# Transposes of the softmax tiles held back by two row tiles instead of one, with a third probability buffer and one bank wait per row tile, in an 8-core attention and FFN layer

## What is computed

```python
xn = layernorm(x)
q_a = rmsnorm(xn @ w_q_a);  q = (q_a @ w_q_b).reshape(s, 16, 128 + 64)
ckv_kpe = xn @ w_kv_a                      # 512 latent + 64 rope
ckv = rmsnorm(ckv_kpe[..., :512]);  k_pe = rope(ckv_kpe[..., 512:])
q_abs = einsum('shd,rhd->shr', q_nope, w_uk)          # 16 heads, 512 wide
scores = (concat(q_abs, rope(q_pe)) @ concat(ckv, k_pe).T) * 192**-0.5
attn = softmax(where(causal, scores, min))
o_ckv = einsum('hqk,kr->qhr', attn, ckv)
y = einsum('qhr,hre->qe', o_ckv, w_uv @ w_o)
out = x + y + (silu(xn @ w_gate.T) * (xn @ w_up.T)) @ w_down.T
```

## Time and profile before

| | us |
|---|---|
| Median of the runs | 7982.84 |
| Lowest and highest of the 2 runs | 7969.11, 7996.58 |
| Profiled execution, its time | 7445.65 |
| Profiled execution, span of the slowest core | 7443.9 |
| Spans of all cores in it | 7394.0 to 7443.9 |
| TensorE matmul, busy in the span | 5451.9 (73%) |
| VectorE, busy | 1725.5 (23%) |
| ScalarE, busy | 1211.8 (16%) |

### The profile page before, as it was taken

One profiled execution on the slowest core, in us unless ns is written; L12 is line 12 of the kernel. 1 busy time (PEld: TensorE's weight loads), 2 busy tenths in 40 slices (PEclk: granted clock), 3 DMA queues, 4 the chain that ended last, 5 costly groups with the idle time before them and its releaser, 6 DMA issues. The chain is left out here.

```text
span 7443.9 us, 70098 instructions; the slowest of 8 cores (7394.0 to 7443.9 us)
## 1 busy us (share of the span) xinstructions
PE 5451.9 (73%) x24376; PEld 2381.6 (32%) x24856; DVE 1725.5 (23%) x4676; ACT 1211.8 (16%) x2788; POOL 366.0 (5%) x408
## 2 busy tenths in 40 slices
PE   3345546666666766667777779976998699869987
PEld 1222222222222222223333334432443244324433
DVE  3323334414332333223333300000000000000000
ACT  0000102213322333223333200000000000000000
POOL 0000002211111010000000000000000000000000
PEclk7666767778888888888888889998999899989999
DMA  3331139998758553453333176645664566446643
GB/s 90 79 62 23 24 57 161 150 134 104 101 80 126 78 80 66 74 103 62 61 61 62 35 178 153 150 127 170 153 153 125 168 153 152 129 158 158 152 130 122
DMA packets 2101325, 819.71 MB, mean 110 GB/s; under 512 B 1819763, under 2 KB 2073844, under 8 KB 2094838
## 3 DMA queue, kind: packets, MB, share of 16 engines
q1 hardware_dynamic: 1621814, 627.20, 33.3%
q0 software_dynamic: 479168, 188.02, 22.3%
HBM read 854.20 MB, written 148.90 MB: 135 GB/s over the span
## 5 line engine op out<-in xcount | busy, mean ns | idle before, releaser
L1040 PE MATMUL ps<-wd,h_sb 128*128 128x512 bf16 x4014 | 930.7, 386 | 236.0 <-DMA wd<-wdown_bf 197.0
L988 PE MATMUL ps<-fx,wg 128*128 128x512 bf16 x4015 | 934.9, 383 | 152.4 <-DMA wg<-wgup_bf 85.1
L764 PE MATMUL ps<-kT,qf 128*128 128x512 bf16 (+3 forms) x2473 | 711.1, 419 | 295.7 <-DVE qf L691 183.1
L996 PE MATMUL ps<-fx,wg 128*128 128x512 bf16 x4013 | 919.7, 379 | 4.4
L1040 PEld LDWEIGHTS ps<-wd,h_sb 128*128 128x128 bf16 x4096 | 394.6, 99 | 772.2 <-issue 348.1
L834 PE MATMUL ps<-ptasm,ckv_nat 128*128 128x512 bf16 (+3 forms) x2502 | 563.2, 389 | 74.8 <-DVE ptasm L725 72.5
L988 PEld LDWEIGHTS ps<-fx,wg 128*128 128x128 bf16 x4096 | 404.1, 99 | 644.0 <-issue 171.2
L1011 DVE TENSOR_TENSOR h_sb<-sil,ps 128x512 bf16<-128x512 f32 x256 | 176.1, 688 | 1801.7 <-PE ps L996 1801.7
L996 PEld LDWEIGHTS ps<-fx,wg 128*128 128x128 bf16 x4096 | 400.8, 98 | 483.3
L800 ACT ACTIVATE p_nat<-s_stage,e_bias 128x512 bf16<-128x512 f32 (+3 forms) x640 | 414.2, 648 | 618.0 <-DVE e_bias L795 618.0
L714 PE MATMUL pt<-ident_sb,p_nat 128*128 128x128 bf16 x2176 | 208.3, 254 | 395.4 <-DVE ptasm L725 298.0
(11 more groups left out here) (102 smaller groups left out, 3082.5 us busy)
## 6 DMA issues: line engine op xcount, KB each, us to landing
wg<-wgup_bf SPq DMA_DIRECT2D x512, 512.0 KB, 4.1
wd<-wdown_bf SPq DMA_DIRECT2D x256, 512.0 KB, 3.9
conv<-wgup POOLq DMA_DIRECT2D x128, 512.0 KB, 10.8
wgup_bf<-conv SPq DMA_DIRECT2D x128, 512.0 KB, 8.2
wo<-wo POOLq DMA_DIRECT2D x16, 2048.0 KB, 23.4
conv<-wdown POOLq DMA_DIRECT2D x64, 512.0 KB, 9.9
wdown_bf<-conv SPq DMA_DIRECT2D x64, 512.0 KB, 6.1
wnope<-wqbnope POOLq DMA_DIRECT2D x64, 384.0 KB, 5.6
```

What stands on the lines that cost most here:

```text
L764: lhs=lhs, rhs=rhs: e.matmul(bank[:, 0:w], lhs(e), rhs(e), start=(cc == 0), stop=(cc == 4)),
L988: b.op("tensor", lambda e, gs=gs, ec=ec, s_g=s_g, pg=pg: e.matmul(pg[:, :], wg_sb[s_g][:, ec * 128:(ec + 1) * 128], xnt_g[gs][:, ec * 512: ...
L996: b.op("tensor", lambda e, gs=gs, ec=ec, s_u=s_u, pu=pu: e.matmul(pu[:, :], wg_sb[s_u][:, ec * 128:(ec + 1) * 128], xnt_g[gs][:, ec * 512: ...
L1040: banks=banks: e.matmul(banks[tt4][:, :], h_sb[:, ic * 512 + tt4 * 128:ic * 512 + (tt4 + 1) * 128], wd_sb[isl][:, (ic % 4) * 512:(ic % 4 + ...
```

## The change

Transposes are now held in a list and emitted when more than two are pending, so those of row tile i-2 stand behind the scores and the scaling of row tile i, and two of them are left for the end of the head. `p_nat` gets a third buffer for that. The three bank waits of a row tile's first three score groups are put together into one, ahead of its first matmul; the fourth group of block 3 keeps its own.

```diff
-            p_nat = [psb(f"p_nat{i}", [128, S], BF16) for i in range(2)]
+            p_nat = [psb(f"p_nat{i}", [128, S], BF16) for i in range(3)]
...
-                    pend_tr = None
+                    pend_tr = []
...
+                        b.waits("tensor", [(V, v_qf), (V, qpeT_ready), (V, kT_ready)]
+                                + [ps_free[1 + (sbank + gg) % 3]
+                                   for gg in range(min(G, 3))])
                         for g in range(G):
                             w = (min(4 * g + 4, n_k) - 4 * g) * 128
                             pk = 1 + (sbank % 3)
                             sbank += 1
                             bank = PS[pk]
-                            b.waits("tensor", [(V, v_qf), ps_free[pk],
-                                               (V, qpeT_ready), (V, kT_ready)])
+                            if g >= 3:
+                                b.waits("tensor", [ps_free[pk]])
...
-                        if pend_tr is not None:
-                            emit_transposes(*pend_tr)
-                        pend_tr = (i, n_k, v_pn)
+                        pend_tr.append((i, n_k, v_pn))
+                        if len(pend_tr) > 2:
+                            emit_transposes(*pend_tr.pop(0))
                     if h < 15:
                         s_qn_tok[1 - hs] = emit_qnope(h + 1)
-                    emit_transposes(*pend_tr)
+                    while pend_tr:
+                        emit_transposes(*pend_tr.pop(0))
```

More of the change, by code:

```diff
@@ L600, in build_nc @@
             ptasm_free = None
-            p_nat_free = [None, None]
+            p_nat_free = [None, None, None]
             qf_free = [None, None]
@@ L715, in emit_transposes @@
                                 PT[pb][:, slot * 128:(slot + 1) * 128],
-                                p_nat[i % 2][:, kc * 128:(kc + 1) * 128], ident[:, :],
+                                p_nat[i % 3][:, kc * 128:(kc + 1) * 128], ident[:, :],
                                 is_transpose=True, start=(slot == 0), stop=last),
@@ L732, in emit_transposes @@
                                 pt_free[pb] = (V, b.cnt[V])
-                        p_nat_free[i % 2] = (T, t_tr_done)
+                        p_nat_free[i % 3] = (T, t_tr_done)
                         pt_evac_v = b.cnt[V]
@@ L796, in build_nc @@
                             e_bias[:, :], mx_row[:, :], -SM, None, ALU.mult), V)
-                        b.waits("scalar", [(V, v_bias), p_nat_free[i % 2]])
+                        b.waits("scalar", [(V, v_bias), p_nat_free[i % 3]])
                         for g in range(G):
@@ L800, in build_nc @@
                             b.op("scalar", lambda e, g=g, w=w, i=i: e.activation(
-                                p_nat[i % 2][:, 4 * g * 128:4 * g * 128 + w],
+                                p_nat[i % 3][:, 4 * g * 128:4 * g * 128 + w],
                                 s_stage[:, 4 * g * 128:4 * g * 128 + w],
@@ L815, in build_nc @@
                         v_pn = b.op("vector", lambda e, n_k=n_k, i=i: e.tensor_scalar(
-                            p_nat[i % 2][:, 0:n_k * 128], p_nat[i % 2][:, 0:n_k * 128],
+                            p_nat[i % 3][:, 0:n_k * 128], p_nat[i % 3][:, 0:n_k * 128],
                             sm_inv[:, :], None, ALU.mult), V)
-                        if pend_tr is not None:
-                            emit_transposes(*pend_tr)
-                        pend_tr = (i, n_k, v_pn)
+                        pend_tr.append((i, n_k, v_pn))
+                        if len(pend_tr) > 2:
+                            emit_transposes(*pend_tr.pop(0))
                     if h < 15:
                         s_qn_tok[1 - hs] = emit_qnope(h + 1)
-                    emit_transposes(*pend_tr)
+                    while pend_tr:
+                        emit_transposes(*pend_tr.pop(0))
                     qf_free[hs] = (T, last_S_T)
```

## The result

| | before | changed |
|---|---|---|
| median of all runs, us | 7690.72 (29 runs) | 7619.57 (30 runs) |
| lowest and highest | 7428.65, 8043.56 | 7487.85, 8131.95 |
| profiled execution, us | 7445.65 | 7496.27 |

The changed kernel takes 1.0083 times as long, 95% interval 1.0071 to 1.0095: slower, by 0.8%, although its median in the table is the lower one. In many executions of either kernel, both runs of before in the table ahead of the prediction among them, the cores of one die or both had a lower clock and took up to 9% longer, so the medians hold a mixture of both kinds, and the ratio leaves such executions out. The predicted ratio, 8059 / 7983 = 1.0095, lies at the upper end of the interval. The predicted time, 8059, was not met: 7619.57 lies outside 7965 to 8165.

A forecast was written before the change was run, and what follows sets the result against it. It took the ScalarE-VectorE ring through s_stage and the copies behind the last scaling to bound attention. Block terms of 10.4 + 12.8 + 28.8 + 24.0 made +76 us, added to 7982.84 for 8059; range 7965 to 8165.

The forecast's parts named there:

- the carry to the median: Whole kernel: the +76 us added unscaled to the timed median 7982.84, giving 8059, though the profiled execution was 7445.65.
- The sum: Attention, 16 heads a block: +0.65, +0.8, +1.8 and +1.5 us a head in blocks 0 to 3, together +76 us.
- Part 1: Scores of row tiles 2 and 3 come earlier: gain of 0.45 us a head in block 0, 0.8 in block 1.
- Part 2: Behind the last scaling, one more transpose-and-copy step: loss of 1.1, 1.6, 1.8, 1.5 us a head in blocks 0 to 3.
- Part 3: Joined bank wait before the scores: taken as 0; at half clock up to 0.8 us a row tile.
- Rival A: Clock swallows the tail: blocks 2 and 3 cost about 0.4 us a head, +36 us, 8019; chance 0.17.
- Rival D: O starts cold and stays so in blocks 2 and 3: +185 us, 8168; sign, granted clock below 0.80; chance 0.13.
- E: Nothing changes, since the new step falls where TensorE or a DMA is late anyway: 7983; chance 0.05.
- B: Copies behind the last scaling are hidden, only the earlier scores count: -30 us, 7953; chance 0.11.
- C: TensorE's waits before the transposes were the bound; all 395.4 us leave the path: 7588; chance 0.03.

The follow-up runs named there:

- e1: Kernel before with the joined bank wait alone: blocks 420, 594, 818 and 1037 us, ratio to before 0.9972 (0.9936 to 1.0009).
- e2: Changed kernel with the bank waits as they were, one ahead of each group: block 2 820 us, ratio to before 1.003 (0.9989 to 1.0071).
- e6: Kernel before with two unused VectorE maxima behind row tile 3's scaling, ahead of T2's copies: ratio to before 1.0046 (1.0019 to 1.0074).
- e3: Kernel before with three p_nat buffers and nothing else: no ratio to before was obtained.
- e7: The e3 kernel once more, against the kernel before: no ratio; blocks 419, 602, 812 and 1040 us on cores 4 to 7.
- e10: e4 with score groups taking turns over five PSUM banks instead of three: block 3 996 us against 1040 in e4; no ratio.
- e9: e4 with the next head's qnope matmuls held until row tile 3's bias in blocks 1 to 3: ratio to before 0.9872 (0.9825 to 0.9919).
- e4: Kernel before with each row tile's transposes and copies emitted behind the next one's bias, not its scaling: ratio to before 0.9897 (0.982 to 0.9973).
- e11: e10 and e9 together, five score banks and held qnope matmuls: block 3 936 us, ratio to before 0.9769 (0.9727 to 0.981).

## Why the prediction was right and wrong

**The time: the step that failed is the carry to the median.** "I carry the +76 over unscaled: 7982.84 + 76 = 8059." The 7982.84 was a median of two runs that both lay over 520 us above the profiled execution, by what I had called something the profile doesn't contain. In 29 runs the median is 7690.72 and the lowest 7428.65. The warning stood in the table: a profiled execution 7% under both timed runs. The range should have reached down to 7445.65 + 76 = 7522 at least.

**The sum.** +76 us predicted; +60 in the blocks, and 0.83% of 7445.65 is 62 (53 to 71 by the interval). So the sum had the right sign and was a quarter too large. Two of its four blocks agree by luck, as its terms show:

- Part 1, the earlier scores: right in kind. Over all cores and heads the score waits had been 1.0 us a head in block 0 and 0.8 in block 1; they are gone, and the rings are 0.5 and 1.0 us shorter. In block 0 I had the ring 1.06 us shorter, with 0.45 of it arriving, which makes the tail 1.7 us longer; it was 0.5 and 1.1, two misses that cancel.
- Part 2, the longer tail: right in kind. It grew by 1.1, 1.3, 1.5 and 2.1 us; I had steps of 1.1, 1.6, 1.8 and 1.5. In block 3 I read the step, 1.54 us, from one head with the transposes at full clock. Over all heads of before that step took 1.74 us; in the changed kernel the new one took 1.79, and the old one 1.95.
- Part 3, the joined wait at 0: right alone (e1), wrong together with the order (e2 against the change: 25 us in block 2). Its own bound, up to 0.8 us a row tile at half clock, is close to what the late heads of block 2 show, 1.0 us in the scores of row tile 2. I put it at nothing because the wait costs nothing at full clock, without knowing at which clock these row tiles run.
- So block 2's +29 against +28 is luck. I had all of it from the tail, and with the longer tail alone (e2) the block was 3 us slower.

**The terms were added as if each microsecond counted once.** e6 shows that one and the same delay costs between a fifth and one and a half times its length, by block. Rival A (the clock swallows the tail) is in part what block 3 does: tail +2.1, O -0.8, block +1.2 a head. A had three quarters of the delay coming back, half of it at O and as much again at the next head's scores, and there nothing came. Rival D (O stays cold for longer) is a small part of block 2: O +0.5 and a clock in it of 0.83 instead of 0.86. Its own sign, a block below 0.80, did not come, and in e2, with T2 in the tail but no joined wait, O did not grow (10.4 us, 10.5 before). I had given A 0.17 and D 0.13 as rivals of the forecast, but they are parts of it, one in each block.

**The other rivals.** E, no change: the ratio's interval excludes it. B, the tail is free: refuted by the result, and by e6, where a delay in the tail alone made the kernel slower by 0.2 to 0.7%. C, the waits before the transposes were the bound: refuted by the result itself, since 67 us of that idle time went and the kernel got slower, and by e3 and e7. (Its time was 7587 by its own terms, not 7588.) The Trainium skill, page "Perfetto Trace Analysis", section "Optimization Strategy", says only that consistent bubbles can mean too little room in SBUF or PSUM. For the gap before the transposes it was not so. For the PSUM banks of the scores in block 3 it was: two more of them took 44 us from the block (e10). The sentence on back-to-back matmuls in the section "Matmul Optimizations" of the same page of the Trainium skill agrees with e9, where O followed denser matmuls and ran at 1.00 instead of 0.78.

## What to carry to other kernels

Before a wait is removed, look who waits for whom at that place: here the bubble before the transposes was the softmax seen from TensorE, and the work put off for its sake landed behind the last scaling, on the way to O. The time in which an engine waits in any case is the better place for it (VectorE's copies during the exponentials, e4). Where dense matmuls follow a pause, try to put work that has to be done anyway right ahead of them, and see that it ends in time: e9 gained 24 and 31 us in blocks 2 and 3 and lost 24 in block 1, where it ended too late. Two pieces that do no harm alone can do harm together (e1, e2), so test them apart and together. And take the time that a change is added to only from runs that agree with the profile.

## What was not expected of the hardware

- A wait that the data does not need made the kernel faster: e9 against e4, 31 us less in block 3 and 24 in block 2, with O at a granted clock of 1.00 instead of 0.78 in the heads shown.
- A delay of 1.27 us a head cost 31 us in block 1 and 5 in block 3 (e6).
- Two gains of 31 and 44 us in block 3 made 104 together (e11).
